# Attention with a mixture-of-experts branch: the experts' turns in twos in the even units, the averages of two units together in the odd ones, a fourth weight buffer

## The chip, the cores and the metric

One core of a Trainium2 chip runs one program. The metric is the device time of one execution in microseconds (us); lower is better. The engines named below are TensorE (PE in the rows, PEld its weight loads), VectorE (DVE), ScalarE (ACT), GpSimd (POOL) and SyncE (SP), which issues nearly all DMAs.

## The reference, cut to what matters

x is 4 x 1024 x 128 in float32. The layer is x + attention(xn) + experts(xn) with xn = layernorm(x):

```python
# attention, 16 heads of 8, T = 1024
s = einsum(q, k); s = s - mean(s); s = s / (mean(|s|) + 1e-6) * score_gain
s = where(causal, s, -1000); r = relu(s) ** 4
y = (r / (sum(r) + 1e-6)) @ v                     # then @ W_proj + b_proj
# experts: 8 of them, the top 2 per token, softmax over the two gate values
x1 = x @ w1 + b1; x2 = x @ w2 + b2
y_e = silu((x1 * x2) @ wg + bg) @ w3 + b3         # weighted and added for the two chosen
```

The mean of |s| needs every score of a row, also those above the diagonal, which the causal part does not use.

## The kernel before, in words

After a prologue (layernorm, q, k, v, the routing), one loop does the rest. It has ALL = 192 units: 16 quads (four heads of one batch entry) of NS = 12 units each. A unit n is one tile of 128 key rows against up to 512 query columns for the four heads of its quad. k = n % 12 is its place in the quad. The widths of the scores at k = 0 to 11 are 512, 384, 256, 128, 512, 512, 512, 512, 512, 384, 256, 128.

Each engine runs its own instructions of unit n in program order, and semaphores join them:

- TensorE (L905 to L947): first the pieces of the unit (L914; score tiles above the diagonal that only feed the mean of |s|), then the four scores (L921), then the unit's expert turns (L924, function `ffn`), then, at the end of the unit, the average of unit n - 2 (L939 to L947, `average`, AVLAG = 2). The average multiplies the weights W and the rectified scores U of four heads into four separate 32-column strips of one bank, in float32: 16 matmul records.
- ScalarE (L762 to L799): at a quad's two column ends the copy of the finished average (L772), the pieces marked A (L780), U = relu(score) for four heads (L788), the turn's evacuations (`evacuate`, L789), and then the squares of W of unit n - 1 that GpSimd does not take (L799).
- VectorE (L1162 to L1180): the pieces marked V (L1169), W = relu(score) * U for four heads (L1177), then the turn's evacuations (L1127 for z, L1135 for the experts' result).
- GpSimd: the causal mask (L660), its share of the squares (L669), and the indirect stores of the experts' rows (L635).

PLAN gives a unit's pieces: at k = 0 to 11 they are VA, VAV, VAV, VAVA, V, V, V, V, VA, VAV, VAV, VAVA. In the first three quads every A is a V.

Banks. PSUM has eight banks: one holds the average, and the other seven (NBANK) go around. `takers` lists, in TensorE's program order, who writes a bank: each piece, each score, two banks for a turn m, one for every other turn. A taker waits (`wait_bank`, L355) until the taker seven places before it has been read for the last time: a score by VectorE's W (L1177), a piece by whoever sums it, m1, ga, gb and tx by ScalarE, m2 and my by VectorE.

Expert turns. The tokens are sorted into NX = 39 tiles of 256 rows, taken in 20 pairs. A pair p has the turns tx (transpose the tokens), m (first two products, one turn per tile), ga and gb (the gate product's two halves, each of both tiles) and my (the last product). `TURNS` lists all 119 in order, and FFN_AT spreads them evenly over units FFN_FROM = 35 to FFN_TO = 180: one turn in a unit, and no turn in about every sixth. SyncE loads a tile's weights (L459, 707 KB) into one of NWB = 3 buffers; tile i waits for turn my of pair (i - 3) // 2 and is issued one unit after it (L467).

U and W have NU = 4 buffers each, freed by the average (`used`).

Of the kernel before, what the change touches and what calls it, by code (L numbers as in the profile page):

```python
# [27 lines left out]
def wait(engine, semaphore, value):  # L28

    if isinstance(value, int) and value <= 0:  # L30
        return
    engine.wait_ge(semaphore, value)


def layer_kernel(nc, x, w_attn, b_attn, w_proj, b_proj, score_gain, gate_w, gate_b, w_expert, out):
    B, T, C = x.shape
    E, _, WW = w_expert.shape
    F = 2 * P
    H = 16
    D = C // H  # L40
    N = B * T
    NT = N // P
# [3 lines left out]
    R = 2 * P  # L46
# [19 lines left out]
    for g in range(4):  # L66
        short = []
        for n in range(TB - 1):
            k, w = P * (n + 1), T - P * (n + 1)
# [19 lines left out]
    for n in range(ALL):  # L89
        for e in plan(n):  # L90
            PIECE_AT[n].append((len(PIECE_COUNT) - 1, e))
            PIECE_COUNT.append({k: v + (k == e) for k, v in PIECE_COUNT[-1].items()})
    assert len(PIECE_COUNT) - 1 == NP * NQ
    PIECE_ENGINE = [e for of_n in PIECE_AT for _, e in of_n]
    SCATTERS = TOPK * NT
    PER_STEP = 2
    POOL_SQUARES = [(1,), (1,), (1,), (1,), (0,), (0,), (0,), (0, 1), (), (1,), (1,), (1,)]
    by_pool = lambda n, p: n * PER_STEP >= SCATTERS and p in POOL_SQUARES[n % NS]
    NU, AVLAG = 4, 2


    NXT, NWB, NYB = 6, 3, 4
    NPAIR = -(-NX // 2)
    tiles_of = lambda p: range(2 * p, min(2 * p + 2, NX))
    TURNS = []
    for p in range(NPAIR):
        TURNS += [("tx", p)] + [("m", i) for i in tiles_of(p)] + [("ga", p), ("gb", p), ("my", p)]
    FFN_FROM, FFN_TO = SCATTERS // PER_STEP + 3, ALL - 12
    FFN_AT, STEP_OF = [[] for _ in range(ALL + AVLAG + 2)], {}
    for k, turn in enumerate(TURNS):  # L110
        STEP_OF[turn] = FFN_FROM + k * (FFN_TO - FFN_FROM) // len(TURNS)
        FFN_AT[STEP_OF[turn]].append(turn)


    NE = B - 1
# [20 lines left out]
    with ctx:  # L136
        def sb(name, shape, dt=F32):
            return ctx.enter_context(nc.sbuf_tensor(name, shape, dt))
# [76 lines left out]
        parts.append(weights.enter_context(nc.sbuf_tensor("parts3", [P, 2, 3, T], BF16)))  # L215
        weights.close()
        gat = sb("gat", [P, 2, NT, C])
        pad = NWB * WW + 2 * (2 * R + 2 * R + 4 * R + 4 * R) - 2 * NT * C
        sb("rest_of_ffn", [P, pad])
        mrow, sums, fw = sb("mrow", [P, 1, H, TB]), sb("sums", [P, 2, P]), sb("fw", [P, 3, P])  # L220
        yT, scale = sb("yT", [P, T]), sb("scale", [P, T])
# [133 lines left out]
        def wait_bank(engine, *who):  # L355

            if PLACE[who] >= NBANK:
                engine.wait_ge(*last_read(takers[PLACE[who] - NBANK]))
# [323 lines left out]
        def _(act):  # L682
# [79 lines left out]
            for n in range(ALL + AVLAG + 2):  # L762
                y = n - AVLAG - 1
                if y >= 0 and y % NS in ENDS:
                    q = y // NS
                    act.wait_ge(used, y + 1)
                    if q == 0:
                        act.wait_ge(part_out[1], 96)
                    if q >= 2:
                        act.wait_ge(y_out[q % 2], 64 * (q // 2) + q % 2)  # L770
                        act.wait_ge(s_out[q % 2], 32 * (q // 2) + q % 2)
                    act.copy(yq[q % 2][:, STEPS[y % NS][0], :], acc).then_inc(acc_ev, 1)  # L772
                if n < ALL:
                    for m, e in PIECE_AT[n]:
                        if e == "A":
                            act.wait_ge(p_ready, m + 1)
                            k_th, at = PIECE_COUNT[m]["A"], 0
                            wait(act, p_used["A"], k_th - 1)
                            for g, _, _, w, col in PIECES[m % NP]:
                                last = act.activation(junk["A"][k_th % 2][:, at:at + w], piece(m)[:, at:at + w], ACT.Relu,  # L780
                                                      accum_out=msum[:, m // NP, g, col:col + 1])
                                at += w
                            last.then_inc(p_used["A"], 1)
                    w = HALF - LOW[n % NS]
                    wait(act, used, n - NU + 1)
                    for g in range(4):
                        act.wait_ge(s_ready, 4 * n + g + 1)
                        act.activation(U[n % NU][:, g, 0:w], score(4 * n + g)[:, 0:w], ACT.Relu).then_inc(u_ready, 1)  # L788
                    for kind, i in FFN_AT[n]:  # L789
                        evacuate(kind, i)  # L790
                y = n - 1
                for p in range(2):
                    if 0 <= y < ALL and not by_pool(y, p):
                        if DIAG[y % NS]:
                            act.wait_ge(w_mask, MASKS[y + 1])
                        else:
                            act.wait_ge(w_done, 4 * y + 2 * p + 2)
                        some = W[y % NU][:, 2 * p:2 * p + 2, 0:HALF - LOW[y % NS]]
                        act.activation(some, some, ACT.Square).then_inc(r_ready[y % NU], 1)  # L799


        @block.tensor
        def _(pe):
# [51 lines left out]
            def average(n, p, of_u):  # L855
                q, (c, j), lo = n // NS, STEPS[n % NS], LOW[n % NS]
                for r in range(2):
                    g = 2 * p + r
                    last = pe.matmul(acc[32 * g:32 * g + VW, lo:HALF],  # L859
                                     usel[:, :] if of_u else VS[q % 2][:, j, g, :],  # L860
                                     (U if of_u else W)[n % NU][:, g, 0:HALF - lo],
                                     start=(j == 0 and of_u == bool(p)), stop=(n % NS in ENDS and of_u != bool(p)),
                                     skip_group_check=True)
                return last
# [40 lines left out]
            for n in range(ALL + AVLAG):  # L905
                q, par = n // NS, n // NS % 2
                if n < ALL:
                    if n % NS == 0:
                        pe.wait_ge(qk_in[par], (q // 2 + 1) * (16 * 5))
                    for m, _ in PIECE_AT[n]:  # L910
                        wait_bank(pe, "piece", m)
                        at = 0
                        for g, t, k, w, _ in PIECES[m % NP]:
                            last = pe.matmul(piece(m)[:, at:at + w], QS[par][in_rows[g % 2], g // 2, P * t:P * (t + 1)],  # L914
                                             KS[par][in_rows[g % 2], g // 2, k:k + w], start=True, stop=True)
                            at += w
                        last.then_inc(p_ready, 1)
                    (c, j), lo = STEPS[n % NS], LOW[n % NS]
                    for g in range(4):
                        wait_bank(pe, "score", 4 * n + g)  # L920
                        pe.matmul(score(4 * n + g)[:, 0:HALF - lo], KS[par][in_rows[g % 2], g // 2, P * j:P * (j + 1)],  # L921
                                  QS[par][in_rows[g % 2], g // 2, HALF * c + lo:HALF * (c + 1)], start=True, stop=True).then_inc(s_ready, 1)
                if n < ALL:
                    for kind, i in FFN_AT[n]:  # L924
                        ffn(kind, i)
                    for b in side(n, S_TURN):
                        pe.wait_ge(m_row, TB * (b + 1))
                        wait_bank(pe, "sums", b)
                        pe.transpose(bank_of("sums", b)[:, 0:P], mrow[:, 0, :, :].rearrange("p h n -> p (h n)"), ident[:, :]).then_inc(ms_t, 1)
                    for c in range(CH):  # L930
                        for b in side(n, S_PROJ + c):
                            pe.wait_ge(yn_ready, b + 1)
                            wait_bank(pe, "proj", CH * b + c)
                            for t in range(TB // CH):
                                at = (c * (TB // CH) + t) * P
                                last = pe.matmul(bank_of("proj", CH * b + c)[:, t * C:(t + 1) * C], yT[:, at:at + P], wp[:, :],
                                                 start=True, stop=True)
                            last.then_inc(proj, 1)
                y = n - AVLAG  # L939
                if y >= 0:  # L940
                    pe.wait_ge(r_ready[y % NU], 2 * (y // NU + 1))
                    if STEPS[y % NS][1] == 0:
                        wait(pe, acc_ev, y // NS * CH + STEPS[y % NS][0])
                    average(y, 0, False)
                    average(y, 1, True)
                    average(y, 0, True)
                    average(y, 1, False).then_inc(used, 1)  # L947
# [298 lines left out]
```

## Time and profile before

| what | value |
|---|---|
| time, median of 3 runs | 894.4 us (892.91 to 896.04) |
| profiled execution, its own time | 888.43 us |
| its span, first to last instruction | 886.7 us |
| PE, DVE, ACT, POOL busy | 84%, 82%, 77%, 70% of the span |
| mean granted TensorE clock | 0.942 of full |

A row of the trace gives the start, the duration, the engine and the line of an instruction or of several of one line; the brackets give the idle time just before it and who ended that. Matmul durations include pipeline time, so a matmul's real hold on TensorE is read from start to next start.

### The profile page before, as it was taken

Reading aid. Unit: us, or ns where it says so; the run is one execution under the profiler, and the core shown is the slowest. Engines: PE = TensorE matmul, PEld = TensorE weight load, DVE = VectorE, ACT = ScalarE, POOL = GpSimd, SP = SyncE. Lnnn points to the kernel's source line nnn. Section 1 sums busy time; section 2 is a strip of 40 time slices with the busy share of each in tenths; the row PEclk is TensorE's granted clock in tenths of the full one; section 3 lists DMA queues with packets and bytes.
Section 4 is the critical chain, followed back from the end, with each engine's and each line's share of the span. In section 5 each row is a group of like instructions: output and inputs, shape, how many; then the busy total and the mean of one; then the engine's idle time right before and its main releaser. Section 6 shows DMA issues by size and latency. Waiting matters only on the chain.

```text
span 886.7 us, 17644 instructions
## 1 busy us (share of the span) xinstructions
PE 740.6 (84%) x5719; PEld 335.2 (38%) x5719; DVE 724.4 (82%) x2043; ACT 683.5 (77%) x1639; POOL 623.9 (70%) x545
## 2 busy tenths in 40 slices
PE   0572888888999999899898989989999999989872
PEld 0530222222444454444344344444434444443222
DVE  7689898989777978786876977787787977778896
ACT  0573888888987878898886787888888887878870
POOL 5262777884897687686876776787777777778773
PEclk9995797979998999999999899999999999999895
DMA  8449703155325304250523423252323605230703
GB/s 270 136 190 264 307 32 85 43 156 156 59 83 167 114 18 131 84 129 19 141 85 59 146 72 70 90 141 85 58 91 99 179 11 141 82 57 10 215 6 101
DMA packets 60330, 97.10 MB, mean 110 GB/s; under 512 B 7360, under 2 KB 39744, under 8 KB 60240
## 3 DMA queue, kind: packets, MB, share of 16 engines
q1 hardware_dynamic: 54544, 86.22, 34.1%
q0 software_dynamic: 4544, 9.38, 3.3%
q8 instruction: 45, 0.74, 0.4%
q10 hardware_dynamic: 1152, 0.40, 0.2%
q14 instruction: 45, 0.37, 0.1%
HBM read 61.29 MB, written 34.36 MB: 108 GB/s over the span
## 4 chain that ended last, share of the span: by engine, by line
PE 45%; DVE 23%; ACT 13%; issue 12%; POOL 4%; DMA 1%; DVEq 1%; SPq 0%; ACTq 0%; POOLq 0%
PE bank L859 19%; DVE W L1177 10%; PE bank L894 7%; ACT U L788 7%; PE bank L874 6%; DVE junk_V L1169 5%; PE bank L914 4%; PE bank L899 3%; ACT W L799 3%; PE bank L921 2%; ACT junk_A L780 2%; POOL W L660 1%; POOL W L669 1%; DVE zT L1127 1%; POOL sorted_x L610 1%
## 5 line engine op out<-in xcount | busy, mean ns | idle before, releaser
L1177 DVE SCALAR_TENSOR_TENSOR W<-bank,U 128x512 f32<-128x512 f32 (+3 forms) x768 | 373.8, 549 | 40.1 <-ACT U L788 38.0
L788 ACT ACTIVATE U<-bank 128x512 f32<-128x512 f32 (+3 forms) x768 | 318.5, 519 | 48.3 <-PE bank L921 35.3
L859 PE MATMUL bank<-W,VS 128*10 128x512 f32 (+3 forms) x1536 | 297.8, 507 | 13.5 <-ACT yq L772 7.2
L859 PE MATMUL bank<-U,usel 128*10 128x512 f32 (+3 forms) x1536 | 292.7, 507 | 0.0
L1169 DVE TENSOR_SCALAR_CACHE_REDUCE junk_V<-bank 128x512 bf16<-128x512 f32 (+3 forms) x445 | 218.3, 533 | 88.2 <-PE bank L914 87.5
L669 POOL TENSOR_TENSOR W<-W 128x1024 f32<-128x1024 f32 (+2 forms) x159 | 231.6, 1460 | 53.9 <-DVE W L1177 45.9
L660 POOL TENSOR_TENSOR W<-W,causal 128x512 f32<-128x512 f32 x128 | 163.6, 1278 | 108.5 <-DVE W L1177 106.9
L799 ACT ACTIVATE W<-W 128x256 f32<-128x256 f32 (+2 forms) x225 | 191.6, 880 | 10.4 <-POOL W L660 10.2
L921 PE MATMUL bank<-QS,KS 48*128 48x512 bf16 (+3 forms) x768 | 162.9, 337 | 39.3 <-DVE W L1177 17.3
L780 ACT ACTIVATE junk_A<-bank 128x512 bf16<-128x512 f32 (+3 forms) x195 | 87.7, 460 | 57.2 <-PE bank L914 56.8
L914 PE MATMUL bank<-KS,QS 48*128 48x512 bf16 (+3 forms) x640 | 102.0, 328 | 17.0 <-DVE junk_V L1169 8.5
L921 PEld LDWEIGHTS bank<-QS,KS 48*128 48x128 bf16 x768 | 56.4, 95 | 110.8 <-DVE W L1177 60.8
L859 PEld LDWEIGHTS bank<-U,usel 128*10 128x10 f32 x1536 | 59.5, 92 | 86.2 <-issue 79.4
L635 POOL DMA_INDIRECT weighted_y<-yb,row_to x78 | 79.3, 1016 | 14.7 <-issue 9.0
L874 PE MATMUL bank<-xT,wb 128*128 128x256 f32 x312 | 82.1, 409 | 7.0 <-DVE junk_V L1169 4.6
L914 PEld LDWEIGHTS bank<-KS,QS 48*128 48x128 bf16 x640 | 29.2, 95 | 153.8 <-issue 109.5
L894 PE MATMUL bank<-zT,wb 128*128 128x256 f32 x312 | 78.8, 396 | 7.6 <-DVE junk_V L1169 5.5
L859 PEld LDWEIGHTS bank<-W,VS 128*10 128x10 f32 x1536 | 59.9, 92 | 66.3 <-issue 36.9
L610 POOL DMA_INDIRECT sorted_x<-xn_row,pos x64 | 62.8, 981 | 18.0 <-issue 14.5
L874 PEld LDWEIGHTS bank<-xT,wb 128*128 128x128 f32 x312 | 58.9, 199 | 24.6 <-issue 16.9
L894 PEld LDWEIGHTS bank<-zT,wb 128*128 128x128 f32 x312 | 57.0, 193 | 24.9 <-issue 13.9
L758 ACT ACTIVATE sT<-bank,wb 128x256 f32<-128x256 f32 x78 | 33.3, 483 | 20.4 <-PE bank L894 20.3
(158 smaller groups left out, 604.5 us busy)
## 6 DMA issues: line engine op xcount, KB each, us to landing
wb<-in_experts SPq DMA_DIRECT2D x39, 707.0 KB
qk_stacked<-parts SPq DMA_DIRECT2D x8, 768.0 KB, 11.7
QS<-qk_stacked SPq DMA_DIRECT2D x32, 192.0 KB
KS<-qk_stacked SPq DMA_DIRECT2D x32, 192.0 KB
xt_all<-sorted_x SPq DMA_DIRECT2D x39, 130.0 KB, 6.0
qk_stacked<-parts SPq DMA_DIRECT2D x8, 512.0 KB, 11.7
gat<-weighted_y SPq DMA_DIRECT2D x8, 512.0 KB, 6.6
sorted_x<-xt_all SPq DMA_DIRECT2D x3, 1300.0 KB, 11.7
```

Of the source, the lines that this page charges most:

```text
L660: pool.tensor_tensor(slot[:, :, 0:P], slot[:, :, 0:P], causal[:, :].unsqueeze(1).to_broadcast([P, 4, P]), ALU.mult).then_inc(w_mask, 1)
L669: pool.tensor_tensor(some, some, some, ALU.mult).then_inc(r_ready[n % NU], 1)
L780: last = act.activation(junk["A"][k_th % 2][:, at:at + w], piece(m)[:, at:at + w], ACT.Relu, accum_out=msum[:, m // NP, g, col:col + 1])
L788: act.activation(U[n % NU][:, g, 0:w], score(4 * n + g)[:, 0:w], ACT.Relu).then_inc(u_ready, 1)
L799: act.activation(some, some, ACT.Square).then_inc(r_ready[y % NU], 1)
L859: last = pe.matmul(acc[32 * g:32 * g + VW, lo:HALF], usel[:, :] if of_u else VS[q % 2][:, j, g, :], (U if of_u else W)[n % NU][:, g, 0:HAL ...
L874: last = pe.matmul(bank_of(part, k)[:, h * R:(h + 1) * R], w[:, at + h * P:at + (h + 1) * P], moving, start=True, stop=True)
L894: last = pe.matmul(to[:, at:at + R], w[:, in_w:in_w + P], zT[k % 2][:, i % 2, h, :], start=(h == 0), stop=(h == 1))
L914: last = pe.matmul(piece(m)[:, at:at + w], QS[par][in_rows[g % 2], g // 2, P * t:P * (t + 1)], KS[par][in_rows[g % 2], g // 2, k:k + w], s ...
L921: pe.matmul(score(4 * n + g)[:, 0:HALF - lo], KS[par][in_rows[g % 2], g // 2, P * j:P * (j + 1)], QS[par][in_rows[g % 2], g // 2, HALF * c ...
L1169: last = vec.tensor_scalar(junk["V"][k_th % 2][:, at:at + w], piece(m)[:, at:at + w], 0.0, None, ALU.max, ALU.add, accum_out=msum[:, m // ...
L1177: vec.scalar_tensor_tensor(W[n % NU][:, g, 0:w], score(4 * n + g)[:, 0:w], 0.0, U[n % NU][:, g, 0:w], ALU.max, ALU.mult).then_inc(w_done, 1)
```

## The change

`GROUPS` replaces `TURNS`: the first turn tx alone, and then for every pair three groups of two: the two turns m; ga and gb; tx of the next pair and my. The 61 groups are spread over units 35 to 180 and each is moved up to an even unit, so that of the 72 even units from 36 to 178 eleven have none: one in each quad from the fifth to the fifteenth (at k = 0 in three quads, at k = 2 in three, at k = 4 in three, at k = 6 in two).

TensorE does the averages in odd units only, two at a time: units n - 3 and n - 2. ScalarE evacuates the first turn of a unit where it did before, and the second one after the squares. The weights get a fourth buffer; a tile's weights now wait for my of pair (i - 4) // 2. `pad` only places later tensors behind the larger buffers.

```diff
-    NXT, NWB, NYB = 6, 3, 4
+    NXT, NWB, NYB = 6, 4, 4
-    TURNS = []
+    GROUPS = [[("tx", 0)]]
     for p in range(NPAIR):
-        TURNS += [("tx", p)] + [("m", i) for i in tiles_of(p)] + [("ga", p), ("gb", p), ("my", p)]
+        GROUPS += [[("m", i) for i in tiles_of(p)], [("ga", p), ("gb", p)], [("tx", p + 1)] * (p + 1 < NPAIR) + [("my", p)]]
     FFN_FROM, FFN_TO = SCATTERS // PER_STEP + 3, ALL - 12
-    for k, turn in enumerate(TURNS):
-        STEP_OF[turn] = FFN_FROM + k * (FFN_TO - FFN_FROM) // len(TURNS)
-        FFN_AT[STEP_OF[turn]].append(turn)
+    for k, group in enumerate(GROUPS):
+        n = FFN_FROM + k * (FFN_TO - FFN_FROM) // len(GROUPS) + 1
+        FFN_AT[n - n % 2] += group
+        STEP_OF.update({turn: n - n % 2 for turn in group})
...
-        pad = NWB * WW + 2 * (2 * R + 2 * R + 4 * R + 4 * R) - 2 * NT * C
+        pad = NWB * (WW + 10) + 2 * (2 * R + 2 * R + 4 * R + 4 * R) - 2 * NT * C
...
-                    for kind, i in FFN_AT[n]:
+                    for kind, i in FFN_AT[n][:1]:
                         evacuate(kind, i)
...
                         act.activation(some, some, ACT.Square).then_inc(r_ready[y % NU], 1)
+                for kind, i in FFN_AT[n][1:]:
+                    evacuate(kind, i)
...
-                y = n - AVLAG
-                if y >= 0:
+                for y in (n - AVLAG - 1, n - AVLAG) if n > AVLAG and n % 2 else ():
                     pe.wait_ge(r_ready[y % NU], 2 * (y // NU + 1))
```

## Rows read from the trace of the kernel before

**Rows 1.** The page, part 1: busy time, share of the span, instructions of each engine

```profile
PE 740.6 (84%) x5719; PEld 335.2 (38%) x5719; DVE 724.4 (82%) x2043; ACT 683.5 (77%) x1639; POOL 623.9 (70%) x545
```

**Rows 2.** Busy time by stretch: PE, PEld, DVE, ACT, POOL (x instructions), PEclk, DMA share, GB/s

```profile
140.00:184.00 44.00, 36.74 (x283) 10.30 (x280) 40.79 (x128) 38.09 (x74) 34.06 (x34) 0.89 0.27 64
...
573.00:621.00 48.00, 44.46 (x368) 21.44 (x364) 39.13 (x108) 41.02 (x106) 35.62 (x30) 1.00 0.37 104
621.00:672.00 51.00, 46.60 (x380) 22.72 (x377) 39.04 (x108) 41.44 (x107) 35.71 (x29) 1.00 0.25 65
```

**Rows 3.** PE's timeline: the first pieces of units 36 and 180

```profile
216.03 0.39 PE L914 MATMUL bank<-KS,QS 48*128 48x512 bf16 x2
...
819.46 0.39 PE L914 MATMUL bank<-KS,QS 48*128 48x512 bf16 x2
```

**Rows 4.** PE's timeline around one full average, units 103 and 104

```profile
501.47 1.99 PE L874 MATMUL bank<-xT,wb 128*128 128x256 f32 x8
503.39 0.60 PE L859 MATMUL bank<-W,VS 128*10 128x512 f32 x2
...
504.27 0.60 PE L859 MATMUL bank<-W,VS 128*10 128x512 f32 x2
504.69 0.60 PE L859 MATMUL bank<-U,usel 128*10 128x512 f32 x2
...
505.23 0.39 PE L914 MATMUL bank<-KS,QS 48*128 48x512 bf16 x2
505.46 0.59 PE L921 MATMUL bank<-QS,KS 48*128 48x512 bf16 x4
505.98 0.48 PE L894 MATMUL bank<-zT,wb 128*128 128x256 f32 x1
```

**Rows 5.** PE's timeline: a turn m with the projection behind it, unit 109

```profile
527.61 1.97 PE L874 MATMUL bank<-xT,wb 128*128 128x256 f32 x8 [0.36 <-DVE junk_V L1169]
529.41 1.05 PE L936 MATMUL bank<-wp,yT 128*128 128x128 f32 x8
```

**Rows 6.** The chain of waits by pieces: start, us, what, count

```profile
516.02 2.02 PE bank L899 x16
...
521.30 1.41 PE bank L859 x16
```

**Rows 7.** Who waited for whom, units 36 to 180: total, times, longest

```profile
DVE junk_V L1169 <- PE bank L914: 78.1, 68, 2.4
...
PE bank L921 <- DVE junk_V L1169: 12.8, 24, 0.5
PE bank L921 <- DVE W L1177: 9.8, 44, 0.3
```

**Rows 8.** VectorE's timeline, units 132 and 133

```profile
621.60 0.69 DVE L1169 TENSOR_SCALAR_CACHE_REDUCE junk_V<-bank 128x512 bf16<-128x512 f32 x1 [0.77 <-PE bank L914]
...
622.91 2.48 DVE L1177 SCALAR_TENSOR_TENSOR W<-bank,U 128x512 f32<-128x512 f32 x4 [0.62 <-ACT U L788]
625.32 0.87 DVE L1127 SCALAR_TENSOR_TENSOR zT<-bank,wb,x 128x256 f32<-128x256 f32 x2
```

**Rows 9.** ScalarE's timeline, the same two units

```profile
622.22 2.05 ACT L788 ACTIVATE U<-bank 128x512 f32<-128x512 f32 x4
624.13 0.87 ACT L750 ACTIVATE x<-bank,wb 128x256 f32<-128x256 f32 x2
...
629.66 1.05 ACT L799 ACTIVATE W<-W 128x1024 f32<-128x1024 f32 x1
```

**Rows 10.** PE's timeline, unit 133: a score and a turn that wait for banks

```profile
626.24 0.33 PE L921 MATMUL bank<-QS,KS 48*128 48x384 bf16 x1 [0.45 <-DVE zT L1127]
626.93 1.97 PE L894 MATMUL bank<-zT,wb 128*128 128x256 f32 x8 [0.36 <-DVE junk_V L1169]
```

**Rows 11.** PE's timeline, unit 50: a turn and an average at the lower clock

```profile
275.19 3.75 PE L874 MATMUL bank<-xT,wb 128*128 128x256 f32 x8 [0.30 <-DVE junk_V L1169]
278.87 1.03 PE L859 MATMUL bank<-W,VS 128*10 128x512 f32 x2
...
281.85 0.61 PE L914 MATMUL bank<-KS,QS 48*128 48x384 bf16 x8
```

**Rows 12.** The first and last of four stretches at 0.5, columns as rows 2

```profile
274.40:281.20 6.80, 6.41 (x22) 3.09 (x26) 3.54 (x11) 3.62 (x10) 6.24 (x7) 0.50 0.73 225
...
677.20:680.50 3.30, 3.30 (x19) 2.10 (x22) 2.24 (x6) 2.35 (x5) 3.05 (x3) 0.50 0.00 0
```

**Rows 13.** PE's and then VectorE's timeline, third quad, no expert turns

```profile
136.42 1.03 PE L859 MATMUL bank<-W,VS 128*10 128x512 f32 x2 [0.69 <-ACT yq L772]
...
139.96 0.51 PE L914 MATMUL bank<-KS,QS 48*128 48x384 bf16 x2
...
140.60 0.56 DVE L1169 TENSOR_SCALAR_CACHE_REDUCE junk_V<-bank 128x384 bf16<-128x384 f32 x1 [2.17 <-PE bank L914]
...
154.40 0.69 DVE L1169 TENSOR_SCALAR_CACHE_REDUCE junk_V<-bank 128x512 bf16<-128x512 f32 x1 [0.62 <-PE bank L914]
```

**Rows 14.** SyncE's own waits, and the DMA issue of the weights

```profile
SPq L459 <- DVE yb L1135: 260.9, 17, 26.9
...
wb<-in_experts SPq DMA_DIRECT2D x39, 707.0 KB
```

More of the change, by code:

```diff
@@ L99, in layer_kernel @@
     NU, AVLAG = 4, 2
-    NXT, NWB, NYB = 6, 3, 4
+    NXT, NWB, NYB = 6, 4, 4
     NPAIR = -(-NX // 2)
     tiles_of = lambda p: range(2 * p, min(2 * p + 2, NX))
-    TURNS = []
+    GROUPS = [[("tx", 0)]]
     for p in range(NPAIR):
-        TURNS += [("tx", p)] + [("m", i) for i in tiles_of(p)] + [("ga", p), ("gb", p), ("my", p)]
+        GROUPS += [[("m", i) for i in tiles_of(p)], [("ga", p), ("gb", p)], [("tx", p + 1)] * (p + 1 < NPAIR) + [("my", p)]]
     FFN_FROM, FFN_TO = SCATTERS // PER_STEP + 3, ALL - 12
     FFN_AT, STEP_OF = [[] for _ in range(ALL + AVLAG + 2)], {}
-    for k, turn in enumerate(TURNS):
-        STEP_OF[turn] = FFN_FROM + k * (FFN_TO - FFN_FROM) // len(TURNS)
-        FFN_AT[STEP_OF[turn]].append(turn)
+    for k, group in enumerate(GROUPS):
+        n = FFN_FROM + k * (FFN_TO - FFN_FROM) // len(GROUPS) + 1
+        FFN_AT[n - n % 2] += group
+        STEP_OF.update({turn: n - n % 2 for turn in group})
+    assert all(len(turns) <= 2 for turns in FFN_AT)
     NE = B - 1
```

## The prediction, made before the changed kernel was run

> **What bounds the kernel now.** I read the page first: four engines are busy 70% to 84% of the span [rows 1], so no single one explains the time. The stretches tell more. In a quad without expert turns VectorE is busy 40.79 of 44 us; in quads with turns TensorE leads (44.46 of 48 and 46.60 of 51), with VectorE and ScalarE at 39 to 41 [rows 2]. The stretch with turns, units 36 to 179, lasts 819.46 - 216.03 = 603.4 us [rows 3], or 50.3 us per quad. The waits of that stretch say what the rest is: VectorE sat 78.1 us before a piece that TensorE had not yet made, and TensorE in turn waited for banks that VectorE had not yet read [rows 7]. So TensorE's program is the longest, and the seven banks, which hold little more than one unit, decide how well the three engines overlap.
>
> **Part 1: averages in twos.** A full average starts at 503.39 and the next piece at 505.23: 1.84 us. Its strips start 0.42 us apart (504.27, 504.69), so four of them are 1.71, and 0.13 is paid once, on the way out [rows 4]. A 384-wide one takes 1.41 [rows 6], again 1.28 and 0.13. Of two averages in one visit one such 0.13 goes: 72 pairs in the stretch with turns give 72 x 0.13 = 9.4 us of TensorE's time. That the second average follows without a gap is shown by no row; between nothing saved (0) and the whole fixed part (0.13) I take 0.13, since strips of one average follow each other without one.
>
> **Part 2: turns in twos.** A turn m with an average behind it takes 503.39 - 501.47 = 1.92 [rows 4]; with the projection behind it, of the same shape as a turn, 529.41 - 527.61 = 1.80 [rows 5]. A turn that is followed by a turn thus saves about 0.1; 119 visits become 61: 58 x 0.1 = 5.8 us. Together 15.2 us, or 1.3 us per quad, if TensorE sets the end everywhere.
>
> The Trainium skill, TensorEngine Tiling (Array Packing), section Key Properties, says that changing the tiling mode drains the array; the 0.13 and 0.1 agree. The same page, section PSUM Bottleneck, speaks against the change: packing quickens TensorE and not the emptying of PSUM. By that rule nothing of the 15.2 us would reach the end, which is the rival of no change below; the trace bears it out in the first three quads, where VectorE leads.
>
> **Part 3: what the pairs do to the banks.** This is the term that decides. With TensorE's order scores, two turns, scores, two averages, it feeds the others in bursts. The units: W for four heads 2.48 us at 512 wide, z for one turn 0.87 (0.83 apart), a V piece 0.61 [rows 8]; U 2.05, x1 0.87, a square of two heads 1.05 [rows 9]; five or six pieces and scores keep TensorE 505.98 - 505.23 = 0.75 us when no bank is missing [rows 4], seven about 0.87 (my estimate, half a slot of 0.21 more). A bank read at time t is written again about 0.05 later, and a matmul's result is picked up 0.4 after its start. I walked one quad of the changed order by hand with these, that of units 132 to 143: ga and gb at k = 0, tx and my at 2, nothing at 4, the two m at 6, ga and gb at 8, tx and my at 10.
>
> - k 0, 1: 0.75 of scores, the turns to 4.45. The last score of k = 1 needs the bank of gb, which ScalarE now reads after a square, at 5.46. Averages of 256 and 128 columns (1.41) to 7.26.
> - k 2, 3: the last score of k = 2 waits for the last W of k = 1 (8.56), tx for a V piece (9.18), tx and my run to 11.75. In k = 3 the third score needs my's bank (12.8) and the last one a V piece behind that (13.5), so scores end at 13.75. Averages of 512 and 384 (3.12) to 16.87.
> - k 4, 5: no turn, so the scores of k = 5 wait for W of k = 4, to 19.75; averages (1.41) to 21.16.
> - k 6, 7: the scores wait for W of k = 5 (to 22.95), the first m for two more banks (23.3), turns to 27.0, the scores for the first z (28.1); averages of 512 and 512 (3.55) to 31.65.
> - k 8, 9: turns to 36.1, scores to 37.45 because of gb's bank, averages to 41.0.
> - k 10, 11: turns to 44.75, scores to 46.75 (my's bank again), averages to 49.87. The copies of the average before U at k = 2 and 6, which ScalarE makes as before, add about 0.2: 50.1.
>
> TensorE's own work in it is 16.1 (averages) + 16.2 (turns) + 9.8 (pieces and scores) = 42.1, so it stands 8.0 us. Scaled to the mean quad, whose turns are 16.5 us by the rows of the turns, it is 50.35 us. Before, with the four stretches at the lower clock taken out (8.8 us, next part), a quad takes (603.4 - 8.8) / 12 = 49.55; 9.8 is its own scores, 17.1 averages and 17.0 turns, so it stands 5.7 us. The saving of 1.3 per quad is there, but the standing grows by 2.2. The places are plain: an even unit without turns has two units' scores (VectorE needs 6 to 7 us for them) in front of one visit of averages, and turns directly followed by scores meet their own banks, which a whole average covered before; now such waits are 0.45 for z and 0.36 for a piece [rows 10]. Net +0.8 per quad, **+9.6 us** in 12 quads. The bound below is the saving alone, -15.2; above, twice the added standing, +2 x 26 - 15 = +37.
>
> **Part 4: TensorE's clock.** At unit 50 a turn took 3.7 us and the average behind it 281.85 - 278.87 = 2.98 in place of 1.92 and 1.84: the granted clock was 0.5 (1.2 GHz) from 274.4 to 281.2, after units with little but waiting scores and a 128-wide average [rows 11]. There are four such stretches in units 36 to 179 [rows 12]; by the same comparison of durations they cost 2.9, 1.4, 2.9 and 1.6, together 8.8 us. After the change the eleven empty even units make such stretches longer (two units' scores, waiting, without an average between them); at about 1.5 us for eight of them it is 12, so **+3 us**, from -8.8 (none) to +10 (all eleven at 1.7).
>
> The Trainium skill, TensorE: Matmul & The Clock Gate, section HAM oscillation, says that waiting between bursts of matmuls brings the clock down again and again; the trace agrees, with 0.5 after such units. It is the page behind the third rival.
>
> **Part 5: the first three quads and the last.** VectorE leads there [rows 2], so a shorter TensorE is worth nothing, and a pair of averages can starve VectorE. When the last score before a pair is written, at most seven banks are unread: 3.0 to 4.3 us of VectorE's work, against 3.12 or 3.55 for a pair plus 0.43 until the next piece arrives. At full clock that costs 0.2 + 0.55 + 0.55 per quad; at 1.2 GHz, as after k = 2 and 6 now (3.54 from 136.42 to 139.96, and VectorE idle 2.17 and 0.62 behind it) [rows 13], a pair costs 1.7 more. Against this goes the wait for ScalarE's copy (0.69 there), which is a unit old when the pair comes. I take +1.3 per quad for three quads, **+4 us**, from 0 to +16, and 0 for the last quad, where ScalarE shares the pieces.
>
> **Part 6, at nothing.** The fourth buffer: no wait of TensorE for weights stands among the waits before, and the weights of a pair are now issued a unit after my of the pair two before it, some nine units (over 30 us) ahead of their turn. SyncE waits in order for my's evacuation (260.9 us in 17 waits) [rows 14]; queued behind it are the next tokens and the next quad's q and k, needed four and nine units later. If the cover failed, each pair would wait one load, some 5 us. U and W: the average of n - 4 is done on TensorE before the scores of n in either order, so NU = 4 holds. ScalarE's second evacuation behind the squares is in the walk. GpSimd's work and order do not change.
>
> **Sum.** +9.6 + 3 + 4 = +16.6 us on the profiled execution's 888.4 us, so 905.0. The runs' median is 6.0 us above that execution, so **911 us**, slower by 1.9%.
>
> **Rivals.**
> - TensorE's saving reaches the end (other sign). Condition: the bursts only move waits that were there already, at most 5.7 us per quad standing as before, and the clock stays as it is. Price: -15.2, so 879; with half the added standing 887. For it: TensorE leads in all twelve quads [rows 2]. Against it: two engines at 39 to 41 of 50 us with one unit's worth of banks. It decides as soon as the added standing is under 1.3 us per quad (I found 2.2). Chance 0.27.
> - The two cancel, within 0.3% (which is about what a measurement of this kernel tells from no change): 892 to 897. The mechanism: VectorE and ScalarE, at 39 to 41 of 50 us, set the pace as soon as TensorE gets shorter, so that its 15.2 us turn into standing and no more; +0.1 per quad. It is what the Trainium skill, TensorEngine Tiling (Array Packing), section PSUM Bottleneck, says of banks that are emptied no faster. Chance 0.08.
> - The clock falls before nearly every pair of averages where VectorE leads: four pairs per quad at 1.7 in four quads is 27 instead of 4 x 2.8 = 11, so +16; eleven empty units +10; with the walk's +9.6 it is +36, so 930. For it stands the clock as it falls now [rows 11 to 13]. Against it: the 3 to 5 us of scores between pairs are half full of matmuls. Chance 0.13.
> - The forecast, 900 to 922: chance 0.52.
>
> The change does what it says by its code; I see no way in which it would not.
>
> **How the numbers follow.** Slower by over 0.3%: 0.52 + 0.13 = 0.65; same 0.08; faster 0.27. The range must reach into the faster case down to 886 (half of it) and up to 928, which leaves out a little under 2 in 10. The forecast's own range is 900 to 922.
>
> **What would show it.** Right: an average pair of 512 + 512 taking 3.55 us and two turns m about 3.7 (parts 1 and 2); scores behind a pair of turns waiting for L758, L1127 or L1135; units 36 to 179 taking 610 to 620 us; the first three quads over 44 us each, with VectorE idle behind L859; more stretches at 0.5. Wrong: a quad with turns under 49 us, the empty even units not showing longer scores, or a wait of TensorE for wb.

## The result and the profile after

The changed kernel takes 939.3 us (937.7 to 940.8) against 893.7 us before: 1.051 times as long, 95% interval 1.048 to 1.054. The profiled execution took 940.2 us, its span is 938.5. The forecast was 911 us in a range of 886 to 928: the sign was right, the size not; the loss is 45.6 us where 17 were forecast.

The page's busy times answer [rows 1]: VectorE, ScalarE and GpSimd work as long as before to within 1.3 us (724.4, 683.5 and 623.9 us there), over a longer span. TensorE is busy 32 us longer with as many instructions, at a mean granted clock of 0.918 in place of 0.942.

```profile
PE 772.8 (82%) x5719; PEld 354.5 (38%) x5719; DVE 723.1 (77%) x2043; ACT 684.6 (73%) x1639; POOL 622.8 (66%) x545
```

Where the 51.8 us of the span lie is read from PE's timeline, at the first pieces of units 0, 36 and 180 (the same points as [rows 3]; unit 0 began at 75.22 before):

```profile
78.19 0.61 PE L918 MATMUL bank<-KS,QS 48*128 48x512 bf16 x2 [7.85 <-DMA VS<-v_stationary]
...
240.62 0.39 PE L918 MATMUL bank<-KS,QS 48*128 48x512 bf16 x2
...
864.37 0.39 PE L918 MATMUL bank<-KS,QS 48*128 48x512 bf16 x2
```

| stretch | before | after | more | forecast |
|---|---|---|---|---|
| before unit 0 | 75.2 | 78.2 | 3.0 | 0 |
| units 0 to 35, no turns | 140.8 | 162.4 | 21.6 | 4 |
| units 36 to 179, turns | 603.4 | 623.8 | 20.3 | 12.6 |
| from unit 180 | 67.2 | 74.1 | 6.9 | 0 |

The 3.0 us ahead of unit 0 are no effect of the loop: two later executions of the kernel before and after began it at 79.12 and 79.34.

By stretch, with the columns of [rows 2]: one quad without turns, the quad of units 120 to 131, and that of units 132 to 143, which the forecast walked through.

```profile
138.28:189.43 51.15, 42.13 (x285) 11.45 (x282) 40.98 (x128) 38.58 (x74) 34.06 (x35) 0.83 0.22 54
609.60:660.64 51.04, 44.95 (x372) 22.70 (x369) 39.47 (x110) 41.40 (x106) 37.91 (x33) 1.00 0.33 99
660.64:709.42 48.78, 44.55 (x372) 22.59 (x369) 38.26 (x106) 40.75 (x106) 34.76 (x30) 1.00 0.29 83
```

A quad without turns needs 51.15 us for the same 41 us of VectorE's work as before in 44, and the granted clock in it is 0.83 where it was 0.89 [rows 2].

What happens there is seen at a pair of averages, PE's timeline and then VectorE's:

```profile
174.63 1.02 PE L863 MATMUL bank<-W,VS 128*10 128x512 f32 x2
174.65 1.02 PE L863 MATMUL bank<-U,usel 128*10 128x512 f32 x2
...
178.48 0.60 PE L863 MATMUL bank<-W,VS 128*10 128x512 f32 x2
...
179.88 0.55 PE L918 MATMUL bank<-KS,QS 48*128 48x512 bf16 x4
...
180.30 0.69 DVE L1172 TENSOR_SCALAR_CACHE_REDUCE junk_V<-bank 128x512 bf16<-128x512 f32 x1 [2.30 <-PE bank L918]
...
189.85 0.69 DVE L1172 TENSOR_SCALAR_CACHE_REDUCE junk_V<-bank 128x512 bf16<-128x512 f32 x1 [2.60 <-PE bank L918]
```

The first rows are matmuls of 1.02 us where they take 0.60 at full clock; the pair lasts 179.88 - 174.63 = 5.25 us in place of 3.55, and VectorE, out of work, waits 2.30 us for the next piece, and 2.60 behind the next pair.

In a unit with turns the same pair runs at full clock, and so do two turns m:

```profile
274.46 3.72 PE L878 MATMUL bank<-xT,wb 128*128 128x256 f32 x16
278.11 0.60 PE L918 MATMUL bank<-KS,QS 48*128 48x512 bf16 x3
...
279.55 0.33 PE L925 MATMUL bank<-QS,KS 48*128 48x384 bf16 x1 [0.45 <-DVE zT L1130]
279.81 0.60 PE L863 MATMUL bank<-W,VS 128*10 128x512 f32 x2
...
283.37 0.55 PE L918 MATMUL bank<-KS,QS 48*128 48x512 bf16 x4
```

Two turns take 278.11 - 274.46 = 3.65 us (two single ones 3.84), two averages 283.37 - 279.81 = 3.56 (two single ones 3.68 [rows 4]). Between them stands the wait for z, as forecast.

### The profile page after: what moved, and what is told of

It is laid out like the page before. It is cut to its first block and busy times, and to the rows that moved or that the text cites. A ratio compares the mean times of both kernels' runs of the same rounds, so it can differ in the third digit from the quotient of the medians.

```text
span 938.5 us, 17644 instructions
## 1 busy us (share of the span) xinstructions
PE 772.8 (82%) x5719; PEld 354.5 (38%) x5719; DVE 723.1 (77%) x2043; ACT 684.6 (73%) x1639; POOL 622.8 (66%) x545
## 5 line engine op out<-in xcount | busy, mean ns | idle before, releaser
L863 PE MATMUL bank<-W,VS 128*10 128x512 f32 (+3 forms) x1536 | 305.9, 545 | 0.0
L863 PE MATMUL bank<-U,usel 128*10 128x512 f32 (+3 forms) x1536 | 303.4, 546 | 0.0
L671 POOL TENSOR_TENSOR W<-W 128x1024 f32<-128x1024 f32 (+2 forms) x159 | 231.3, 1458 | 75.2 <-DVE W L1180 67.3
L925 PE MATMUL bank<-QS,KS 48*128 48x512 bf16 (+3 forms) x768 | 179.6, 338 | 67.1 <-DVE W L1180 34.7
L918 PE MATMUL bank<-KS,QS 48*128 48x512 bf16 (+3 forms) x640 | 113.4, 329 | 27.7 <-DVE junk_V L1172 15.9
L863 PEld LDWEIGHTS bank<-U,usel 128*10 128x10 f32 x1536 | 73.0, 99 | 98.8 <-issue 92.7
L863 PEld LDWEIGHTS bank<-W,VS 128*10 128x10 f32 x1536 | 73.0, 99 | 79.3 <-issue 70.9
L878 PE MATMUL bank<-xT,wb 128*128 128x256 f32 x312 | 73.8, 389 | 6.8 <-DVE junk_V L1172 5.9
L918 PEld LDWEIGHTS bank<-KS,QS 48*128 48x128 bf16 x640 | 31.9, 94 | 124.4 <-issue 70.5
L898 PE MATMUL bank<-zT,wb 128*128 128x256 f32 x312 | 72.4, 385 | 3.6 <-DVE junk_V L1172 2.7
L878 PEld LDWEIGHTS bank<-xT,wb 128*128 128x128 f32 x312 | 58.2, 192 | 20.8 <-issue 13.6
L782 ACT ACTIVATION_READ_ACCUMULATOR junk_A<-bank 128x1 f32 x195 | 42.0, 216 | 0.0
```

The costliest lines, as they stand in the source:

```text
L671: pool.tensor_tensor(some, some, some, ALU.mult).then_inc(r_ready[n % NU], 1)
L863: last = pe.matmul(acc[32 * g:32 * g + VW, lo:HALF], usel[:, :] if of_u else VS[q % 2][:, j, g, :], (U if of_u else W)[n % NU][:, g, 0:HAL ...
L878: last = pe.matmul(bank_of(part, k)[:, h * R:(h + 1) * R], w[:, at + h * P:at + (h + 1) * P], moving, start=True, stop=True)
L898: last = pe.matmul(to[:, at:at + R], w[:, in_w:in_w + P], zT[k % 2][:, i % 2, h, :], start=(h == 0), stop=(h == 1))
```

## The experiments

Each ratio is against the kernel before, run beside the experiment on the same chip. The chips differ: that kernel took 909.2 us beside the first four experiments, 907.8 beside the next three, 895.2 beside the filler on the kernel before and the two runs with six banks, and 906.5 beside the second filler. The loss differs too: 1.051 on the first chip, but 1.043 and 1.042 on the two on which the kernel before takes 907 to 909 us. The first four experiments belong to the chip with 1.042, and are read against that.

### Turns in twos alone

```diff
-                for y in (n - AVLAG - 1, n - AVLAG) if n > AVLAG and n % 2 else ():
+                for y in (n - AVLAG,) if n >= AVLAG else ():
```

> The changed kernel with the averages one per unit again (two units behind, as before): turns in twos and the fourth buffer stay. Theory A (the pairs of averages cost: they starve VectorE and let TensorE's clock fall where there are no turns): within 5 us of before, so 889 to 899. Theory B (turns directly followed by scores meet their own banks, and this is what costs): 10 to 20 us over before, 904 to 914.

Measured: 933.7 us, ratio 1.025 (1.020 to 1.031), so some 23 us over the 909.2 beside it. Theory A in this plain form falls: without any pair of averages more than half of the loss on this chip (1.042) is there. It is also a little more than the 10 to 20 us of theory B. Two turns with an average behind them are one stretch without scores, from 693.55 to 699.01, and VectorE waits behind it:

```profile
693.55 3.69 PE L898 MATMUL bank<-zT,wb 128*128 128x256 f32 x16 [0.30 <-DVE W L1180]
697.17 0.60 PE L863 MATMUL bank<-W,VS 128*10 128x512 f32 x2
...
699.01 0.60 PE L918 MATMUL bank<-KS,QS 48*128 48x512 bf16 x3
...
699.43 0.69 DVE L1172 TENSOR_SCALAR_CACHE_REDUCE junk_V<-bank 128x512 bf16<-128x512 f32 x1 [2.57 <-PE bank L918]
```

That wait stands at full clock, but the clock has a large part in this run as well. Units 36 to 179 took 631.6 us with 61 us at 0.5; the kernel before, traced on the other of the two slower chips, took 609.0 with 24. Seven pairs of turns took 5.0 to 6.5 us in place of 3.65. If I compare each turn and average with its like at full clock, the lower clock costs about 24 us here and 10 there, so my estimate is that 14 of these 23 us are the clock. No run separates the two.

### Averages in twos alone

```diff
-                y = n - AVLAG
-                if y >= 0:
+                for y in (n - AVLAG - 1, n - AVLAG) if n > AVLAG and n % 2 else ():
```

(on the kernel before, with its single turns and three buffers)

> The kernel before with the averages of two units together in the odd units, and nothing else: one turn per unit, three buffers. Theory A: nearly the whole loss, 930 to 942 us, and the first three quads at 51 us each as in the changed kernel. Theory B: the first three quads still at 51 (they have no turns, +22 us and +7 in the last), but nothing added in units 36 to 179, so 915 to 925.

Measured: 1026.4 us, ratio 1.128 (1.123 to 1.133). Both theories missed by far. The first three quads took what both expected (52 us and more), but units 36 to 179 took 710 us, of which 130 at 0.5. A turn in an odd unit now stands ahead of the pair, and here it starts at the lower clock, behind scores that waited for banks:

```profile
646.55 3.24 PE L874 MATMUL bank<-xT,wb 128*128 128x256 f32 x8 [0.36 <-DVE junk_V L1168]
649.72 0.97 PE L859 MATMUL bank<-W,VS 128*10 128x512 f32 x2
...
653.63 0.55 PE L914 MATMUL bank<-KS,QS 48*128 48x512 bf16 x4
...
654.06 0.69 DVE L1168 TENSOR_SCALAR_CACHE_REDUCE junk_V<-bank 128x512 bf16<-128x512 f32 x1 [3.35 <-PE bank L914]
```

From 646.55 to 653.63 TensorE makes no score, 7.1 us. VectorE stood 166 us before pieces in units 36 to 179, in place of 79 in the kernel before on the other slower chip. By the same comparison of durations the lower clock makes up nearly half of the 101 us by which this stretch is longer than there. So the costs of the two halves of the change don't add: alone they are 2.5% and 12.8%, together 4.2% on this chip. My reading is that the pairing of turns takes the turns out of the odd units and thereby makes room for the pairs of averages. The longest stretch between two units' scores fits that: at full clock 1.92 + 1.84 = 3.8 us before, 3.65 and 3.56 in the change, 5.5 with turns alone in twos and 5.5 with averages alone in twos. At the lower clock it is 6.7 before (281.85 - 275.19 [rows 11]) and 7.1 in the rows above. How much of each loss is this length and how much the clock was not separated by a run.

### Averages in twos only beside turns, and only where the even unit has turns

The first keeps single averages before unit 36 and from unit 180; the second keeps them in every even unit without turns, by the condition `n % 2 or n >= ALL or not FFN_AT[n]`.

```diff
+    AV_AT, done = [[] for _ in range(ALL + AVLAG)], 0
+    for n in range(ALL + AVLAG):
+        if n % 2 or n < FFN_FROM or n >= FFN_TO:
+            AV_AT[n] = list(range(done, max(done, n - AVLAG + 1)))
+            done = max(done, n - AVLAG + 1)
...
+                for y in AV_AT[n]:
```

> The changed kernel, with the averages in twos only in units 36 to 179; before and behind one per unit. Both theories: the first three quads return to 44 us and the last to its old length, which gives back 21.6 + 6.9 us: 911 us. If it gives back under 15 us, the loss there is not due to the pairs but to something that comes with the change from the start.

> The changed kernel, with one average at the end of every even unit that has no turn (the odd unit behind it then has one as well); pairs only where the even unit before has turns. Theory A: the stretches at the lower clock in units 36 to 179 go back to four or fewer, so besides 28.5 us also most of 9.5 us comes back: 898 to 904 us. Theory B: as the kernel with pairs in units 36 to 179, 908 to 912.

Measured: 930.0 us, ratio 1.023 (1.018 to 1.028), and 918.3 us, ratio 1.010 (1.007 to 1.013). On this chip the changed kernel was run later, at 945.2 us and 1.042. Against that the first gives back 2.0 points, 15 to 18 us, where I expected 28.5, and with 15 as my border for another cause. The place is as expected: beside that later trace units 0 to 35 take 152.0 us in place of 162.4 and the last quad 66.6 in place of 73.0, while units 36 to 179 stay (628.5 and 628.3). The size is not: the second and third quad return to 49.0 and 46.7 us, not to 44. The kernel before is itself longer there on such a chip (last section).

The second gives another 1.3 points, the share of the eleven empty even units, but not by the clock, as theory A had it: in units 36 to 179 there are still 11 stretches at 0.5, not four or fewer (48 us, 51 in the first of the two kernels). What did fall is TensorE's waiting for a bank that VectorE's W frees, from 20.3 to 14.8 us. The rest, 1.0%, is not attributed: the pairs of turns, the pairs of averages beside them, the fourth buffer and a low clock are all left in it.

### A filler that keeps TensorE at work

The kernel before and the changed one ran again on one chip, and beside them the changed kernel with matmuls of noughts where even units have no turns.

> The kernel before once more, for its trace on the same chip as the runs beside it. The chip of the runs before this one gave 909 us for it in place of 894; if that is the granted clock, the stretches at 0.5 are more here than in the first trace where the time is higher, and the quads without them are as long as there.

> The changed kernel once more, as the reference for the next run on the same chip. 1.05 times before, as on the first chip; if the ratio is under 1.03 here, the loss hangs on the chip's clock more than on the order of the work.

```diff
+            pool.memset(nought[:, :], 0.0)
...
+                if 4 <= n < ALL and n % 2 == 0 and not FFN_AT[n]:
+                    fresh = (n - AVLAG - 1) % NS in ENDS
+                    if fresh:
+                        pe.wait_ge(acc_ev, (n - 3) // NS * CH + STEPS[(n - 3) % NS][0] + 1)
+                    for g in (0, 2, 1, 3, 0, 2, 1, 3):
+                        pe.matmul(acc[32 * g:32 * g + VW, 0:HALF], nought[:, :], sel[:, 0:4, :].rearrange("p a c -> p (a c)"),
+                                  start=fresh, stop=False, skip_group_check=True)
```

> The changed kernel, with one 512-wide average of noughts (zero weights, 1.7 us of matmuls) added at the end of every even unit without turns, so that TensorE is kept at work there; the sums stay the same. Theory C (the lower clock makes the pairs 5.2 us long where there are no turns): pairs there return to 3.55 us and the first three quads from 51 to 46 to 47 us, 15 to 25 us under the changed kernel beside it. Theory D (the length of a pair starves VectorE at any clock): the pairs get shorter, but the added 1.7 us is a stretch without scores too, and the quads stay at 50 us or more, within 6 us of the changed kernel or slower.

Measured: the changed kernel 947.5 us, ratio 1.043 (1.035 to 1.050); with the filler 922.9 us, ratio 1.016 (1.009 to 1.023). More work on TensorE takes 24.6 us off. The mean granted clock goes from 0.909 to 0.960.

In total this is what theory C expected, by place it is not. The wide pairs of the second and third quad do return to 3.13 to 3.56 us, and only 10 us there are at 0.5 in place of 38. But these quads take 51.1 and 50.2 us, where theory C said 46 to 47 and theory D 50 or more. Units 0 to 35 gain 7.0 us (164.7 to 157.7), units 36 to 179 with their eleven fillers 13.6, the last quad 4.6. So the clock's part of the loss is shown, and what holds the quads without turns at 50 us is taken up with the second filler below.

The kernel before, in the one execution on this chip, took 912.7 us. Its quads with turns are mostly as long as in the first trace (48.3, 50.6, 50.9 us for the three quads of units 120 to 155, the same to 0.1), but units 0 to 35 take 155.6 us, not 140.8. That is only partly the clock: see the last section. My expectation of it was half right.

In the first filler TensorE waited for ScalarE's copy at k = 2 and 6; a second one puts it there into the next odd unit, ahead of the scores, and ran beside the changed kernel again.

> The changed kernel once more, beside the next run. Over before by 1.04 to 1.05.

> The changed kernel with averages of noughts in the even units without turns, as in the run with the filler before, but where the copy of a finished average would be waited for (k = 2 and 6) the filler stands in the next odd unit, ahead of the scores. Theory C: the first three quads at 45 to 47 us each in place of 51, no pair of averages above 3.6 us there, 25 to 35 us under the changed kernel beside it, which leaves 10 to 20 over before for the banks. Theory D: under 10 us gained.

Measured: the changed kernel 945.2 us, ratio 1.042 (1.038 to 1.047); with this filler 926.1 us, ratio 1.020 (1.015 to 1.024). It takes 19.1 us off, which is between the two theories. The two fillers thus take back 24.6 of 39.7 and 19.1 of 38.7 us, their own matmuls included: the clock carries half of the loss or somewhat more, and the rest stays. Two waits of VectorE behind pairs in a quad without turns, with the pair that ends at 228.47 in full (units 33 to 36):

```profile
224.92 0.60 PE L865 MATMUL bank<-W,VS 128*10 128x512 f32 x2
...
228.47 0.55 PE L925 MATMUL bank<-KS,QS 48*128 48x512 bf16 x4
...
228.90 0.69 DVE L1184 TENSOR_SCALAR_CACHE_REDUCE junk_V<-bank 128x512 bf16<-128x512 f32 x1 [0.61 <-PE bank L925]
236.75 0.69 DVE L1184 TENSOR_SCALAR_CACHE_REDUCE junk_V<-bank 128x512 bf16<-128x512 f32 x1 [0.90 <-PE bank L925]
```

The pair is 3.55 us here and the waits 0.61 and 0.90, against 5.25, 2.30 and 2.60 for the same two places of the quad in the changed kernel. So of each of these waits 1.7 us is the clock, and 0.6 to 0.9 the length of the pair at full clock. Behind the pair at k = 3 it is more: 1.56 us at full clock, against 2.92 in the changed kernel.

Theory C also said 45 to 47 us for these quads. The quad of units 12 to 23 had the full clock throughout and still took 50.3 us. Its sums, with the columns of [rows 2], and a row of VectorE in it, behind a stop that no engine of the program ended ("remote"):

```profile
136.62:186.94 50.32, 43.23 (x382) 12.24 (x380) 40.98 (x128) 38.08 (x74) 34.20 (x35) 1.00 0.22 55
...
171.43 0.69 DVE L1184 TENSOR_SCALAR_CACHE_REDUCE junk_V<-bank 128x512 bf16<-128x512 f32 x1 [4.12 <-remote]
```

Without these 4.1 us the quad would take 46.2, as theory C has it. That is a subtraction and not a run: such stops stand in the kernel before too on this kind of chip (last section), and no filler was run with the change on a chip without them.

### Narrow averages in twos

```diff
...
+        if n % NS not in (0, 4) or n >= ALL:
+            AV_AT[n] = list(range(done, max(done, n - AVLAG + 1)))
+            done = max(done, n - AVLAG + 1)
...
+                for y in AV_AT[n]:
```

(on the kernel before)

> The kernel before with only the narrow averages in twos: those of k = 10 and 11 together in the unit k = 1 of the next quad, those of k = 2 and 3 together at k = 5; the others one per unit. These pairs take 1.42 us, less than one full average. Theory D: nothing starves, and twice 0.13 us per quad is saved: 0 to 4 us faster than before. Theory C: the even units left without an average let the clock fall at k = 1 and 5 as often as in the changed kernel, 5 to 15 us slower than before.

Measured: 921.9 us, ratio 1.016 (1.009 to 1.024), 14 us slower. The size is that of theory C, but the cause is not shown to be the clock. Units 0 to 35 lost nothing (155.1 us, the kernel before on this chip 155.6); units 36 to 179 took 621.1 in place of 609.0. There it had 34 us at 0.5 in place of 24, which by the durations of turns and averages costs 5 of the 12 us. Two rivals stand beside the clock and are not separated from it. ScalarE waited 16.7 us for finished averages before its copy, in place of 3.2, since a pair ends later than a single one. And at k = 0 and 4 a turn is now followed by scores directly.

### The filler on the kernel before

```diff
+            pool.memset(nought[:, :], 0.0)
...
+                if 4 <= n < ALL and n % NS in (1, 5) and all(kind == "tx" for kind, _ in FFN_AT[n]):
+                    for g in (0, 2, 1, 3, 0, 2, 1, 3):
+                        pe.matmul(acc[32 * g:32 * g + VW, 0:HALF], nought[:, :], sel[:, 0:4, :].rearrange("p a c -> p (a c)"),
+                                  start=False, stop=False, skip_group_check=True)
```

> The kernel before, with one 512-wide average of noughts ahead of the average at k = 1 and at k = 5, in units without a turn or with tx alone; nothing else changed. Theory C (the clock falls where scores wait between narrow averages, and the time follows it): fewer stretches at 0.5, the slow averages at k = 2 and 6 of the first quads back to 1.84 us, 6 to 15 us faster than before. Theory D (only the length of the stretches without scores counts, the clock is a companion): no gain, 0 to 5 us slower.

Measured: 889.6 us against 895.2, ratio 0.995 (0.993 to 0.998). It beats the kernel before by 0.5%, a little less than theory C expected. The averages at k = 2 in the second and third quad are back to 1.84 us, those at k = 6 take 2.47 and 1.84 in place of 2.92 and 2.69. A quad without turns, and units 36 to 179:

```profile
129.80:173.10 43.30, 35.88 (x316) 10.36 (x312) 40.86 (x129) 37.70 (x75) 33.85 (x34) 0.96 0.26 64
218.00:819.00 601.00, 553.62 (x4537) 266.18 (x4533) 481.36 (x1320) 498.10 (x1280) 451.92 (x388) 1.00 0.32 89
```

The clock is at 1.00 throughout the units with turns, without the four stretches of [rows 12], and the quad has 0.96 in place of 0.89 [rows 2]. That gives 2.3 us in 603.4 and 0.7 us in that quad. My reading: each of the seven fillers in units 36 to 179 takes 1.7 us of TensorE where it leads, and in that quad VectorE is the bound and had only 3.2 us of standing to lose.

### A bank less

```diff
-    NBANK = 7
+    NBANK = 6
```

> The changed kernel with six banks going around in place of seven. If its bursts live on the banks' stock (theory D, and part 3 of the prediction), a bank less costs it some 0.6 us per stretch without scores, two stretches in each of 96 pairs of units: 60 to 110 us over the changed kernel. Theory C: 20 to 40 us.

> The kernel before with six banks. It has one long stretch without scores per turn and a short one in units without: by theory D a bank less costs it about as much as it costs the changed kernel in the units with turns and far less in the others, 40 to 70 us over before, and less than the changed kernel loses.

Measured: the changed kernel with six banks 982.8 us, ratio 1.100 (1.096 to 1.104); the kernel before with six banks 941.9 us, ratio 1.052 (1.048 to 1.055). The changed kernel with seven banks was not run on this chip; with the first chip's 1.051, on which the kernel before takes about as long (894 and 895 us), a bank is worth about 45 us to each (1.100 against 1.051 is 4.9 points, 1.052 against 1 is 5.2). With the 1.042 of the slower chips it would be 5.7 against 5.2. Both programs live on the stock of banks, and that the change leans on it much more, as theory D asked, is not seen. The loss of about 44 us lies between the 20 to 40 of theory C and the 60 to 110 of theory D, so this pair of runs decides for neither.

## Why the prediction was wrong, point by point

**The savings of parts 1 and 2: right.** A pair of averages saves 3.68 - 3.56 = 0.12 us (forecast 0.13), a pair of turns 3.84 - 3.65 = 0.19 (forecast 0.1). TensorE's program did get shorter, in units 36 to 179 by 72 x 0.12 = 8.6 us and by up to 58 x 0.19 = 11.0 us.

**The walk of part 3: right in the mean, but not in its own quad.** The quad of units 132 to 143, in which the clock stayed at 1.00, was walked to 49.87, with the copies 50.1 us. Its first pieces, PE's timeline at units 132, 136, 138 and 144:

```profile
660.64 0.39 PE L918 MATMUL bank<-KS,QS 48*128 48x512 bf16 x2
...
677.08 0.33 PE L918 MATMUL bank<-KS,QS 48*128 48x384 bf16 x1
...
681.57 0.39 PE L918 MATMUL bank<-KS,QS 48*128 48x512 bf16 x1
...
709.42 0.39 PE L918 MATMUL bank<-KS,QS 48*128 48x512 bf16 x2
```

These are 16.44, 20.93 and 48.78 us; the walk had 16.87, 21.16 and 49.87. Units 36 to 179 without what the lower clock costs (about 16 us, by the same comparison of durations as for [rows 11]) take 623.8 - 16 = 608, before 594.6: about +13, forecast +9.6. Where scores follow turns directly they wait for z or my, and an even unit without turns saves little: both were seen.

The agreement of the mean is in part luck. The quad that I walked took 50.6 us before and 48.8 after: it became 1.8 us shorter where the mean was to become 0.8 longer. Other quads at full clock made up for it, units 120 to 131 with 51.0 in place of 48.3 and units 156 to 167 with 52.0 in place of 50.1. A quad with turns under 49 us was one of my own signs of being wrong, and it came, and units 36 to 179 left the 610 to 620 us that I named. One quad scaled to twelve was too thin a base for a difference of 0.8 us.

**Part 4, the clock in units with turns: mis-sized.** Nine stretches at 0.5 in place of four; they cost 16 - 8.8, some 7 us, where +3 was forecast. I counted one average at 1.7 for an empty unit; at unit 87 it was a pair of 512 and 384 that took 5.76 in place of 3.13. Two turns at unit 102 look dearer still, 7.5 us in place of 3.65, but most of the excess is a wait for a bank between the two, which belongs to part 3:

```profile
528.14 1.97 PE L878 MATMUL bank<-xT,wb 128*128 128x256 f32 x8 [0.30 <-DVE W L1180]
532.51 3.19 PE L878 MATMUL bank<-xT,wb 128*128 128x256 f32 x8 [2.41 <-DVE junk_V L1172]
535.63 0.60 PE L918 MATMUL bank<-KS,QS 48*128 48x512 bf16 x1
```
What the clock cost was set by the length of the work that followed, and the change puts its longest pieces of work right behind its weakest stretches.

**Part 5, the quads without turns: the step that failed.** Forecast +4 us for three quads and 0 for the last; measured 21.6 and 6.9. I had the mechanism and priced it for the places that were slow before (k = 2 and 6), at +1.3 per quad. In fact all four wide pairs of a quad run largely at 0.5 (4.6 to 5.3 us each). Before, with an average in every unit, the clock was at 1.00 at k = 8 to 11; now the even ones have none, two units of waiting scores stand in its place, and the pairs at k = 9 and 11 ran at a mean of 0.65 to 0.68. This was the third rival, whose price for all these quads was 16 us (measured 28.5) and for which I gave a chance of 0.13, on the ground that the scores between pairs are half full of matmuls. The ground was wrong. The price was too low as well, by the starving at full clock: 0.6 to 1.6 us behind a wide pair where I had 0.2 to 0.55.

How the 21.6 us split is an estimate: by the durations of the averages 11 of them are the clock, and about 5 of the 6.9 in the last quad. Of the whole loss the fillers took back 19 to 25 us out of about 39 on the slower chips. The 21.6 us belong to the first chip. On one of the slower ones the same two kernels differ by 9.1 us in units 0 to 35 (164.7 and 155.6), because the kernel before has stops there that it lacks on the first.

The Trainium skill, TensorE: Matmul & The Clock Gate, section "A second HAM failure mode: psum-queue depth-cycling", tells of a kernel that cycles through PSUM banks, in which TensorE idles for short times between groups of matmuls so often that the clock goes up and down. The trace agrees: TensorE was busy 42.1 of 51.15 us in the quad at 0.83, its longest wait there was 1.01 us, and ahead of the slow pair at 174.63 it waited five times for 0.2 to 0.3 us. I had weighed only the section on waits between bursts, and this one speaks for the third rival in the four units k = 8 to 11.

**Part 6: right as far as is known.** No wait of TensorE for weights stands in the trace after. The fourth buffer was not run by itself. The copy of the average is no longer what a pair waits for.

**The rivals.** That the saving reaches the end, and that the two cancel, are both out by the result. Turns alone in twos, with single averages, are a loss as well (ratio 1.025), in which banks and clock both have a part. The first rival's line has a slip: with half the added standing the saving of 15.2 us leaves 892 us, not 887, which is half the saving.

## What to carry to other kernels

When three engines are within a fifth of each other and share a few banks, look at the longest stretch in which the producing engine makes nothing for the others, and compare it with the work that the banks can hold; a switch saved was worth 0.1 to 0.2 us here, a starved consumer 0.6 to 3. Where TensorE waits for banks, an interleaved piece of matmul work can do a second job, as the two fillers did here, which is to keep its clock up: before moving it, see what is left in the weakest stretch, and which work comes right behind. Judge two halves of such a change together: here one alone was more than half as bad as both (2.5% of 4.2%), the other three times as bad (12.8%). And when a program is run on several chips, read each experiment against the changed kernel on the same chip, and by stretch: a total can meet a theory that its parts don't.

## What the runs showed of the hardware that was not expected

Adding work can help: 512-wide matmuls of noughts, with nothing to compute, raised the mean granted clock from 0.909 to 0.960 and took 24.6 us off the changed kernel, and 5.5 us (0.5%) off the kernel before.

The same program was 1.5% slower on other chips (909 and 907 against 894 us), and the profile puts most of it into units 0 to 35, which took 155.6 us in place of 140.8. Besides more time at 0.5 (66 us of it, before 46) the trace shows stops of ScalarE and VectorE that no engine of the program ended, in the kernel before on that chip:

```profile
DVE junk_V L1169 <- remote: 10.3, 3, 4.5
ACT U L788 <- remote: 6.5, 4, 3.4
```

There is no such wait in the first trace. All of them lie in units 0 to 35. What holds the engines there was not found. With them the kernel before loses time in these units that it doesn't lose on the first chip, which fits the smaller ratios of the change there, 1.042 and 1.043 in place of 1.051.
